# Two-block conditional MLP with adapter: adapter products of blocks 0 to 2 from float32r parts

## The reference

```python
# layer 0: conditional gated MLP
scale = cond @ norm_w.T + 1.0
h = x * (scale * rsqrt(mean(x*x) + 1e-6))
u = h @ up_w.T                       # 512 -> 2 * 2048
val, gate = split(u)
h = val * gelu(gate)
hq = act_quant(h)                    # per token, 127 levels by its largest |h|
wq = weight_quant(down_w)            # -1, 0, 1 by the mean of |w|
x = hq @ wq.T + x
# layer 1: conditional adapter, 512 -> 128 -> 512
Wd_b = Wd + 0.1 * (cond @ Wdd.T + bdd)     # per batch
Wu_b = Wu + 0.1 * (cond @ Wdu.T + bdu)
down = relu(x @ Wd_b.T + bd)         # the adapter's down product
out = x + down @ Wu_b.T + bu         # the adapter's up product
```

## Time and profile before

| what | value |
|---|---|
| median of three runs | 840.19 us |
| profiled execution | 839.96 us |
| its span in the trace | 838.2 us |
| PE busy | 823.3 us, 98% |
| DVE busy | 661.7 us, 79% |
| ACT busy | 397.4 us, 47% |
| DMA, mean | 223 GB/s |
| granted TensorE clock | 1.000 |

### The profile page before, as it was taken

How to read it: one execution, slowest core, us unless ns; L and a number is a source line. 1 busy time by engine, 2 the same in 40 slices (tenths; PEclk the granted TensorE clock), 3 DMA queues, 4 the chain that set the end, 5 groups by cost and what they waited for, 6 DMA issues and landing times.

```text
span 838.2 us, 11811 instructions
## 1 busy us (share of the span) xinstructions
PE 823.3 (98%) x3902; PEld 358.0 (43%) x3902; DVE 661.7 (79%) x964; ACT 397.4 (47%) x649; POOL 119.9 (14%) x91
## 2 busy tenths in 40 slices
PE   6999999999999999999999999999999999999998
PEld 4334444444444434444444444444444444444443
DVE  5997887989878889767777678988975666675986
ACT  5778887766455532227445543326433333324000
POOL 0363332302001053200101011100200000001000
PEclk9999999999999999999999999999999999999999
DMA  9879988666999862378798866337247444435232
GB/s 345 337 263 346 341 292 297 234 219 221 307 346 372 322 215 107 138 258 281 277 327 306 299 222 190 115 93 259 86 127 232 138 129 155 137 95 176 101 126 75
DMA packets 64859, 186.64 MB, mean 223 GB/s; under 512 B 7072, under 2 KB 8352, under 8 KB 64416
## 3 DMA queue, kind: packets, MB, share of 16 engines
q1 hardware_dynamic: 64512, 185.63, 63.9%
q10 hardware_dynamic: 288, 0.26, 0.1%
HBM read 154.41 MB, written 30.41 MB: 220 GB/s over the span
## 4 chain that ended last, share of the span: by engine, by line
PE 90%; DVE 2%; issue 2%; DVEq 0%
PE b_ps L1326 9%; PE b_ps L1328 9%; PE b_ps L1330 9%; PE a_ps L1326 6%; PE aux_ps L1381 6%; PE a_ps L1328 6%; PE a_ps L1330 6%; PE aux_ps L1439 6%; PE aux_ps L1526 3%; PE aux_ps L1517 3%; PE c_ps L1326 3%; PE e_ps L1328 3%; PE e_ps L1326 3%; PE e_ps L1330 3%; PE c_ps L1328 3%; PE c_ps L1330 3%
## 5 line engine op out<-in xcount | busy, mean ns | idle before, releaser
L1917 DVE SCALAR_TENSOR_TENSOR h_ring<-v_sb,unscale,gelu 128x512 f32<-128x512 f32 x63 | 55.1, 874 | 67.5 <-issue 35.4
L1326 PE MATMUL b_ps<-t_mov,u_l 128*128 128x512 f16 x252 | 95.5, 379 | 2.7 <-DVE c_ps L1878 2.7
L1330 PE MATMUL b_ps<-t_mov,u_l 128*128 128x512 f16 x252 | 95.5, 379 | 0.0
L1328 PE MATMUL b_ps<-t_mov,u_l 128*128 128x512 f16 x252 | 95.5, 379 | 0.0
L1941 DVE TENSOR_TENSOR hmax<-gelu,hmax 128x512 f32<-128x512 f32 x120 | 88.6, 740 | 7.8 <-ACT gelu L1090 2.9
L1060 ACT ACTIVATE b_ps<-a_ps 128x512 f32<-128x512 f32 x63 | 36.7, 582 | 99.1 <-PE a_ps L1330 99.1
L1094 ACT ACTIVATE gelu<-h_ring 128x512 f32<-128x512 f32 x64 | 40.3, 630 | 65.8 <-DVE h_ring L1917 65.8
L1976 DVE TENSOR_TENSOR h_ring<-h_ring,qscale 128x1024 f16<-128x1024 f32 x48 | 64.7, 1388 | 0.0
L1076 ACT ACTIVATE gelu<-a_ps,unscale 128x512 f32<-128x512 f32 x64 | 43.7, 682 | 43.4 <-DVE hmax L1941 41.1
L908 POOL PARTITION_ALL_REDUCE yscale<-hmax x8 | 17.9, 2267 | 321.4 <-DVE hmax L1941 320.7
L1090 ACT ACTIVATE gelu<-h_ring 128x512 f32<-128x512 f32 x64 | 40.2, 628 | 45.6 <-DVE h_ring L1927 45.3
(11 more groups left out here) (253 smaller groups left out, 1690.3 us busy)
## 6 DMA issues: line engine op xcount, KB each, us to landing
w_ring<-in_Wdu SPq DMA_DIRECT2D x64, 512.0 KB, 6.2
w_ring<-in_Wdd SPq DMA_DIRECT2D x56, 512.0 KB, 7.2
u_l<-ul_dram SPq DMA_DIRECT2D x48, 512.0 KB, 4.7
u_e<-ue_dram SPq DMA_DIRECT2D x48, 384.0 KB, 3.2
h_ring<-in_up_w SPq DMA_DIRECT2D x16, 512.0 KB, 6.5
x_sb<-in_x SPq DMA_DIRECT2D x8, 1024.0 KB, 8.2
res<-in_down_w SPq DMA_DIRECT2D x16, 512.0 KB, 7.4
ul_dram<-u_l SPq DMA_DIRECT2D x15, 512.0 KB, 5.7
```

The lines of the kernel that those rows point to most:

```text
L1326: pe.matmul(ps[:, :], weight(n, p, 0, k), hi, start=fresh and k == 0, stop=False, skip_group_check=True)
L1328: pe.matmul(ps[:, :], weight(n, p, 0, k), lo, start=False, stop=False, skip_group_check=True)
L1330: mm = pe.matmul(ps[:, :], weight(n, p, 1, k), hi, start=False, stop=k == 1, skip_group_check=True)
L1917: dve.scalar_tensor_tensor(out=h_slot(n)[:, TB:TS], in0=val[:, :], scalar=unscale[:, s // 2, j:j + 1], in1=gelu2[:, :], op0=ALU.mult, op1= ...
```

## The change

Six things are changed together.

1. New SBUF tensors of type float32r, laid over `res` (`up_parts`, four of 128x512), over `stage` (`mid_parts`) and over `x_sb` (`x_parts`), which are free in that stretch.
2. At the end of ACT's quad 46 `up_weight_high` writes the high parts of the two batch 0 adapter weights to `up_parts`. It waits for the stores from `res`. At the end of `val2(47)` DVE's `up_weight_low` writes the low parts.
3. For blocks 0 to 2 the relu goes back into its PSUM bank, a second activation writes its high part to `mid_parts`, and DVE's `mid_low` the low part, first thing in the quad that follows.
4. For blocks 1 and 2 ACT's `x_high` (end of quads 50 and 53) and DVE's `x_low` (quads 51, 52 and 54, 55) split the adapter's input.
5. The up products of blocks 0 to 2 and the down products of blocks 1 and 2 become three float32r matmuls each instead of one f32 matmul: 12 and 8 of them.
6. The last two blocks' x goes to `x_sb` at quads 56 and 57 instead of 50 and 53, `load_c11` of quad 58 waits for the last up product of block 2, and `keep_p1` of the last round waits for it with both halves. A few semaphores are merged (the same events are counted on a shared one).

```diff
+LAST_X = {56: 0, 57: 1}
+SPLIT = len(MID_AT)
+MID_SPLIT = {1: (50, (51, 52)), 2: (53, (54, 55))}
...
+        with ExitStack() as first:
+            up_parts = first.enter_context(nc.sbuf_tensor("up_parts", [P, 4, TB], F32R))
+            mid_parts = first.enter_context(nc.sbuf_tensor("mid_parts", [P, 2, TB], F32R))
+            x_parts = first.enter_context(nc.sbuf_tensor("x_parts", [P, 2, KD, TB], F32R))
+        res = sb("res", [P, 4, TB])
+        stage = sb("stage", [P, 2, TB])
+        x_sb = sb("x_sb", [P, 2, KD, TB])
...
             def load_c11(d):
+                if d == 2:
+                    aux_ready(sp, "up", SPLIT - 1, KD - 1)
...
             def load_x(s, t):
-                if s:
+                if s == NSB:
+                    aux_ready(sp, "mid", max(MID_SPLIT))
+                elif s:
                     sp.wait_ge(s_tlo, 7 * s + 1)
...
-                if j in NEXT_X:
+                if s + 1 < NSB and j in NEXT_X:
                     load_x(s + 1, NEXT_X[j])
+                if n in LAST_X:
+                    load_x(s + 1, LAST_X[n])
...
                 act.wait_ge(s_x_c22, 2 if at < 3 else 4)
-                act.activation(stage[:, at % 2, :], bank("mid", i)[:, :], ACT.Relu,
+                if at >= SPLIT:
+                    act.activation(stage[:, at % 2, :], bank("mid", i)[:, :], ACT.Relu,
+                                   bias=bd_sb[:, 0:1]).then_inc(s_relu, 1)
+                    return
+                act.activation(bank("mid", i)[:, :], bank("mid", i)[:, :], ACT.Relu,
                                bias=bd_sb[:, 0:1]).then_inc(s_relu, 1)
+                act.wait_ge(s_relu, at + 1)
+                if at:
+                    aux_ready(act, "up", ADAPTERS[at - 1], KD - 1)
+                act.activation(mid_parts[:, 0, :], bank("mid", i)[:, :], ACT.Copy)\
+                    .then_inc(s_part_hi, 1)
+
+            def up_weight_high():
+                act.wait_ge(s_l1w, 3)
+                for h in range(2):
+                    act.wait_ge(s_res_put[h], 16 * 6)
+                    act.wait_ge(s_c22_put[h], 16)
+                act.activation(up_parts[:, 0, :], l1_wu[:, 0, :], ACT.Copy).then_inc(s_part_hi, 1)
+                act.activation(up_parts[:, 2, :], l1_wd[:, 0, :, :].rearrange("p k n -> p (k n)"),
+                               ACT.Copy).then_inc(s_part_hi, 1)
+
+            def x_high(i):
+                act.wait_ge(s_ad[i % 2], 16 * (i // 2 + 1))
...
+                for half in range(2):
+                    rows = slice(2 * half, 2 * half + 2)
+                    act.activation(x_parts[:, 0, rows, :], ad_slot(i)[:, rows, :], ACT.Copy)\
+                        .then_inc(s_x_hi, 1)
...
+                if n == NQ - NP - 2:
+                    up_weight_high()
...
+                if i in MID_SPLIT:
+                    for k in range(KD):
...
+                        pe.matmul(ps[:, :], hi, x_hi, start=(k == 0), stop=False)
+                        pe.matmul(ps[:, :], hi, x_lo, start=False, stop=False)
+                        mm = pe.matmul(ps[:, :], lo, x_hi, start=False, stop=(k == KD - 1))
+                    mm.then_inc(s_aux, 1)
+                    return
...
+                if at < SPLIT:
+                    pe.wait_ge(s_part_lo, 2)
+                    pe.wait_ge(s_part_lo, at + 3)
+                    cols = slice(P * k, P * k + P)
+                    pe.matmul(ps[:, :], up_parts[:, 0, cols], mid_parts[:, 0, :],
+                              start=True, stop=False)
+                    pe.matmul(ps[:, :], up_parts[:, 0, cols], mid_parts[:, 1, :],
+                              start=False, stop=False)
+                    pe.matmul(ps[:, :], up_parts[:, 1, cols], mid_parts[:, 0, :],
+                              start=False, stop=True).then_inc(s_aux, 1)
+                    return
...
+            def up_weight_low():
+                dve.wait_ge(s_part_hi, 1)
+                dve.tensor_tensor(up_parts[:, 1, :], l1_wu[:, 0, :],
+                                  up_parts[:, 0, :].bitcast(F32), ALU.subtract)\
+                    .then_inc(s_part_lo, 1)
...
+            def mid_low(i):
+                dve.wait_ge(s_part_hi, ADAPTERS.index(i) + 3)
+                dve.tensor_tensor(mid_parts[:, 1, :], bank("mid", i)[:, :],
+                                  mid_parts[:, 0, :].bitcast(F32), ALU.subtract)\
+                    .then_inc(s_part_lo, 1)
...
                 val2(n)
+                if n == NQ - NP - 1:
+                    up_weight_low()
```

More of the change, by code:

```diff
@@ L9 @@
 F32 = mybir.dt.float32
+F32R = mybir.dt.float32r
 F16 = mybir.dt.float16
@@ L262, in build @@
         h_ring = sb("h_ring", [P, SLOTS, TS])
-        x_sb = sb("x_sb", [P, 2, KD, TB])
-        res = sb("res", [P, 4, TB])
         wq = sb("wq", [P, NP, D], F8)
@@ L270, in build @@
         v_sb = sb("v_sb", [P, TB])
-        stage = sb("stage", [P, 2, TB])
         l1_wd = sb("l1_wd", [P, B, KD, BN])
@@ L494, in build @@
         s_out = sem("s_out")
+        s_x_hi = sem("s_x_hi")
+        s_x_lo = sem("s_x_lo")
+        s_part_hi = sem("s_part_hi")
+        s_part_lo = sem("s_part_lo")
         s_dabs = sem("s_dabs")
-        s_dsum = sem("s_dsum")
         s_stat1 = sem("s_stat1")
@@ L527, in bank_free @@
                 "p5": (s_x1, 2 * KD * i + 6 + key[-1] + 1),
-                "mid": (s_relu, at + 1),
+                "mid": (s_part_lo, at + 3) if at < SPLIT else (s_relu, at + 1),
                 "up": (s_out, KD * at + key[-1] + 1),
@@ L568, in put_sums @@
             def put_sums():
-                sp.wait_ge(s_sums_lo, 2)
+                sp.wait_ge(s_first_lo, 3)
                 sp.dma_start(ue_dram[0].rearrange("p (a m) -> p a m", a=2)[:, :, 256:768],
@@ L885, in weight_sums @@
                     if j == 6:
-                        pool.wait_ge(s_sums_lo, 2)
+                        pool.wait_ge(s_first_lo, 3)
                     pool.wait_ge(s_ulo, part_count(j - 2, 3))
@@ L1021, in sums_high @@
                 act.activation(s_split(pair)[:, 0, :], s_sum(0, 2 * pair, 2 * pair + 2), ACT.Copy,
-                               scale=um_mul[:, 0:1]).then_inc(s_sums_hi, 1)
+                               scale=um_mul[:, 0:1]).then_inc(s_first_hi, 1)
             def first_val_high():
@@ L1114, in keep_p1 @@
                     else:
-                        aux_ready(act, "up", (2, 1)[h], KD - 1)
+                        aux_ready(act, "up", SPLIT - 1, KD - 1)
                     act.activation(kept1(h), bank("c11", d, h)[:, :], ACT.Copy)\
@@ L1244, in _ @@
                     stage_group(g)
+                if n == NQ - NP - 2:
+                    up_weight_high()
+                for i, (at, _) in MID_SPLIT.items():
+                    if n == at:
+                        x_high(i)
                 if n in MID_AT:
@@ L1304, in product @@
                     if n - 1 == MEAN_QUAD:
-                        pe.wait_ge(s_mean, 1)
+                        pe.wait_ge(s_mean, 2)
                     ps = e_ps
@@ L1495, in down_total @@
             def down_total():
-                pe.wait_ge(s_dsum, 1)
+                pe.wait_ge(s_mean, 1)
                 pe.matmul(e_ps[:, 0:1], ones[:, :], dsum[:, :], start=True, stop=True)\
@@ L1513, in adapter_mid @@
                     pe.wait_ge(s_ad[i % 2], 16 * (i // 2 + 1))
+                if i in MID_SPLIT:
+                    for k in range(KD):
+                        if k % 2 == 0:
+                            pe.wait_ge(s_x_lo, 2 * i - 1 + k // 2)
+                        hi, lo = (up_parts[:, 2 + n, P * k:P * k + P] for n in range(2))
+                        x_hi, x_lo = (x_parts[:, n, k, :] for n in range(2))
+                        pe.matmul(ps[:, :], hi, x_hi, start=(k == 0), stop=False)
[3 more added lines that the diff above has]
+                    return
                 for k in ks:
@@ L1523, in adapter_up @@
                 ps = take("up", i, k)
+                at = ADAPTERS.index(i)
+                if at < SPLIT:
[9 more added lines that the diff above has]
+                    return
                 if k == 0:
-                    pe.wait_ge(s_relu, ADAPTERS.index(i) + 1)
+                    pe.wait_ge(s_relu, at + 1)
                 pe.matmul(ps[:, :], l1_wu[:, i // 4, P * k:P * k + P],
@@ L1709, in sums_low @@
             def sums_low(pair):
-                dve.wait_ge(s_sums_hi, pair + 1)
+                dve.wait_ge(s_first_hi, pair + 2)
                 split = s_split(pair)
@@ L1714, in sums_low @@
                                          scalar=um_mul[:, 0:1], in1=split[:, 0, :],
-                                         op0=ALU.mult, op1=ALU.subtract).then_inc(s_sums_lo, 1)
+                                         op0=ALU.mult, op1=ALU.subtract).then_inc(s_first_lo, 1)
             def first_val_low():
@@ L2077, in residual, with x_low @@
                     dve.tensor_tensor(xk, y, xk, ALU.add).then_inc(s_x1, 1)
+            def up_weight_low():
```

(27 more changed lines are left out.)

6 lines of the change are left out of this document (4 added, 2 removed).

## The result

Eight runs of the changed kernel have a median of 843.50 us (841.99 to 845.02), eight of the one before 840.26. The ratio is 1.0037, 95% interval 1.0027 to 1.0047: slower by 3.1 us (2.3 to 3.9). The forecast was 842.3 and slower by 2.1. The profiled execution took 845.02 us with a span of 843.3, 5.1 more than before; 1.2 of them were there before the first changed instruction (`gate1(46)` at 570.18 against 569.01), so they are no part of it: 0.9 of them stand already at `gate1(0)` (30.31 against 29.44), and in the profiles of the experiments `gate1(46)` starts anywhere from 568.25 to 570.24.

What follows compares the result with a forecast made beforehand. PE was taken to bound the kernel: 839.96 - 4.2 (passes) + 5.8 (superblock change: 4.5 wait, 1.3 subtractions) + 0.5 (quad 50) = 842.1, plus 0.2 to the median, 842.3 us. Its own range was 841.4 to 843.3, the wider one 838.0 to 845.5.

Steps and rivals of the forecast that it cites:

- The bound: Whole kernel: PE, busy 98% and 90% of the chain, passes on added work or waits one for one.
- The wait of `up_weight_high`: ACT, quad 46: stands from 569.7 to 574.3 for stores from `res`; DVE's run starts 4.5 us late, PE follows.
- `up_weight_low`: DVE behind `val2(47)`: two subtractions in a run without idle time, nothing hides them, 1.3 us added.
- `mid_low(0)`: DVE, quad 50: 0.6 us more before `seed_c(50)`, with 0.1 us of room, costs PE 0.5 us.
- The passes: PE, 20 up and down products: three float32r passes of 0.216 us replace 0.857 us each, giving back 4.2 us.
- The rival of the dearer pass: PE: float32r passes cost more than f16; 855.2 us at 0.43, 853.8 at 0.406, 844.3 at 0.25; chance 0.12.
- `x_high`, `x_low`, the SP steps: ACT, DVE and SP, from quad 50 on: splitting x and moved loads cost nothing; quad 51 is the tightest.
- The growing lateness: Rival: DVE's lag meets `x_low` in quad 51, the clock drops or ACT falls behind; 843.8 to 845.3 us, chance 0.10.
- Two of its signs: Signs of the growing lateness in the trace after: PE waits in quads 51 to 57, or a granted clock under 1.

Runs made afterwards that it cites:

- the two experiments that take it away: Changed kernel with weights split in quad 48 instead of 46 and 47: 837.54 us; changed kernel with quad 46's stores issued ahead of its weight loads: 838.36 us.
- the store experiment: Changed kernel with SP issuing the stores of quad 46 ahead of that quad's weight loads instead of behind them: 838.36 us, ratio 0.9978.
- the wait alone: Kernel before, with only ACT's wait for the stores from `res` added at the end of quad 46: 844.54 us, ratio 1.0054.
- its own experiment: Kernel before, with only two 128x512 subtractions added on DVE behind `val2(47)`: 841.04 us, ratio 1.0014.
- the experiment with 256 columns: Kernel with weights split in quad 48 and `mid_low(0)` behind `seed_c(50)`, its down products of blocks 1 and 2 done in two 256-column halves: 837.50 us.

## Why the prediction was right, and where its sizes were off

- **The bound.** PE one for one, with the question who is late where: right. Without the one wait the sign turns (837.54 and 838.36 us, the two experiments that take it away; the second takes away nothing else). The forecast's own range, 841.4 to 843.3, just misses the 843.50 measured.
- **The wait of `up_weight_high`.** Right in place, releaser and carrying. For the 4.5 us put on DVE's run 5.35 were found in the profiled execution; 0.5 of the difference is the landing, 6.2 us after issue and not 5.7. By the ratios the wait with the copies is worth 4.9 us (the store experiment), and the wait alone, without copies, 4.5 (3.1 to 6.0).
- **`up_weight_low`.** 1.3 forecast, 1.2 by trace and by its own experiment. That PE pays for all of it was read from the earlier trace rows: not from the share of busy time but from a run without idle that ends where PE waits.
- **`mid_low(0)`.** 0.5 forecast, 0.49 measured by starts. From `gate1(46)` to p7(50) all terms together are 7.0 where 6.3 was forecast; the wait makes up the whole of that.
- **The passes.** Mis-sized. 4.2 us was the forecast and 3.2 is measured, because the distance of f16 passes was taken for float32r ones. This one term is as large as the whole distance between the forecast (2.1) and the result (3.1). That is in part luck: the other terms together were 0.7 over the forecast in the profiled execution, which is 1.5 us above the median. In the median the wait was some 0.4 over (4.9 for 4.5), which the intervals don't tell from nothing. The rival of the dearer pass names 0.25 us and 844.3, and the truth lies between it and the forecast, but for another reason than its load: the experiment with 256 columns took that away. The rule of the Trainium skill (TensorE: Matmul & The Clock Gate, The mechanism) that a load overlaps matmuls only in another row group doesn't hold here: loads of 98 ns in f16 and of 190 ns in float32r lie inside distances of 0.216 and 0.231 us, full tiles both. The same section of the Trainium skill also lets a load into a background weight buffer be pulled ahead of running matmuls, and with that the trace agrees.
- **`x_high`, `x_low`, the SP steps.** Nothing forecast, nothing found; quad 51 was tight as said.
- **The growing lateness.** Two of its signs came about and cost little: the granted clock (below), and a wait of PE behind quad 57, which cost less than 0.2 us.

A version with a lower time than both kernels came out: weights split in quad 48, `mid_low(0)` behind `seed_c(50)`, 836.88 us, and 836.60 with f16 parts.

## What to carry to other kernels

Before an instruction goes into an engine's list, look up when each thing it waits for is done, and what stands behind it; here a copy of 0.6 us stood still for 5 us in front of the one activation that PE needed next, on an engine busy less than half of the time. An average share of busy time says nothing of a stretch: find the run without idle, and see whether it ends at a wait of the engine that bounds. Here the place of the work was worth more than the work: 5.6 us between the two places, where the passes give 3.2.

## What the hardware showed that was not expected

**The clock, hidden.** PE's 3.5 us of idle was followed by half clock. In windows of 2 us (columns: length, busy of PE, PEld, DVE, ACT, POOL with counts, granted clock, DMA share, GB/s):

```profile
576.00:578.00 2.00, 0.12 (x1) 0.13 (x2) 0.00 (x0) 1.90 (x4) 0.00 (x0) 1.00 1.03 373
578.00:580.00 2.00, 2.00 (x6) 0.74 (x5) 1.22 (x1) 2.00 (x3) 0.00 (x0) 0.53 0.81 314
580.00:582.00 2.00, 2.00 (x7) 0.73 (x6) 1.18 (x2) 1.11 (x3) 0.00 (x0) 0.62 0.39 110
582.00:584.00 2.00, 2.00 (x11) 0.92 (x10) 1.72 (x4) 1.78 (x3) 0.00 (x0) 1.00 0.69 220
```

A granted clock of 0.53 and 0.62 over four microseconds is the level of 1.2 GHz for most of it, and PE did 2 x (0.47 + 0.38) = 1.7 us less than it could. Six of the eight runs have a mean clock of 0.997 to 0.999, two have 1.000; the two, 843.13 and 842.75, are not clearly faster. The reason is in the rows of DVE above: DVE was late anyway, and had waited for PE's p4(46) only 0.18 us when its run began, so by these rows all but some 0.2 us of the slow clock lay in time in which PE would have waited. The kernel with the wait alone bears this out: PE's gap was 2.9 us, the clock stayed at full speed in its profile, and PE waited 0.40 and 0.59 us at p7(47) and p5(48), where the changed kernel, slowed, shows no wait.

**The landing of a store.** The same pair of 256 KB stores took 2.3 us when issued ahead of the weight loads of the quad, and 5.7 to 6.5 us behind them (0.9 MB), with 2 MB of `load_ad` issued 1.3 us after the second store. Which of these transfers makes the difference no run tells apart. A landing time read at one place doesn't move with the instruction.
